# Attention multiplied in place in the sums' banks, the FFN's residual in halves, and the second load of x issued one batch ahead

## The chip, the cores and the metric

The kernel runs on one core of one Trainium2 chip. Its metric is the device time of one launch in microseconds (us), the median of three runs. Besides, one launch was recorded by the profiler, and all the rows in this document come from such recorded executions. The engines are called PE (TensorE, matrix products), DVE (VectorE), ACT (ScalarE), POOL (GpSimd) and SP (SyncE, which here only issues transfers). SBUF is the on-chip memory for operands. PSUM holds the matrix products, in 8 banks of 128 x 512 float32 values each.

## The reference: what is computed

One transformer layer on 32 batches of 512 tokens with 256 features: linear attention with 16 heads, and then a feed-forward network (FFN) with quantized weights. Each half has a layer norm in front and a residual around it. Cut to what matters:

```
q, k = elu(xn @ Wq.T + bq) + 1, elu(xn @ Wk.T + bk) + 1     # xn = layernorm(x)
v    = xn @ Wv.T + bv
num  = masked(q @ k.T) @ v + q @ S          # within chunks of 128, plus the state S so far
den  = sum(q * (cumsum(k) + z))             # per head and token
x1   = x + (num / den) @ Wo.T + bo
y    = silu((layernorm(x1) * gamma + beta) @ w1 + b1)        # w1, w2 dequantized; 256 -> 1024
out  = x1 + 0.5 * (y @ w2 + b2)                             # 1024 -> 256
```

## The kernel before, in words

One loop iteration works on three batches at once: the attention of batch i, the projections (k, q, v and the denominators) of batch i + 1, and the FFN of batch i - 1. The layer norm of batch i + 2's input is prepared too. Iterations 1 to 29 are a hardware loop; iterations 0, 30, 31 and 32 stand beside it as straight code with parts left out (32 is the last FFN alone).

Each engine has its own program, written out by hand as a list of calls: `pe_iteration`, `ve_iteration`, `ac_iteration`, `po_iteration` and `sp_iteration`. An engine carries its list out strictly in order. Between engines, an `Event` is a semaphore counted up when an instruction is done, and `w.need(event, shift, k)` makes the next instruction wait for that event of the batch `i + shift`. The order on each engine and these waits are all that sets the time.

Every matrix product is split into high and low parts, to be exact in float32: for an operand, ACT makes the high part (`..._hi`, a copy to the type FP32R) and DVE or POOL the low part (`..._lo`, the difference). Each stage passes through a PSUM bank. Which one is in the table `BANKS` (one entry per use, in TensorE's order). `free_bank` makes PE wait until the last use of the same bank has been read, and `FREED_BY` says by what.

The steps that the change and the prediction speak of:

- **Attention.** PE sums `num` in banks 0 and 1 (`values`, `from_states`). `reciprocals` makes 1/den, and eight transfers by SP (`sp_reciprocals`, L1049) spread it over the partitions into `rb` in SBUF. `attention(t)` (L662, DVE) multiplies `num` by `rb` and writes `rb`, once for each half t. `attention_hi` (L916, ACT) and `attention_lo` (L705, DVE) split the product into `gt_hi` and `gt_lo`, the operands of the output projection.
- **FFN.** For each of the eight column blocks j: `ffn_scaled` (L830, ACT) and `ffn_sum` (L626, DVE) read two banks, `ffn_silu` (L838, ACT) applies silu, `ffn_hi` (L845, ACT) makes `s_hi`, and `ffn_lo` (L986, POOL) makes `s_lo`. The second product `fc2` waits for all eight `s_hi` and `s_lo`.
- **The FFN's residual.** `residual` (L683, DVE, four instructions) makes `res` from `x1`, `residual_bias` (L998, POOL) adds the bias, and `final` (L673, DVE) adds the product and writes `out_t`.
- **The input a second time.** SP loads batch i again (L1057) into `xb` once the old `x1` is complete. `input_bias` (L992, POOL) adds the bias of the output projection, and `add_residual` (L714, DVE) makes `x1`.
- **Norms.** `ve_norm_x` (L563 to L570, DVE) makes the statistics of the input for batch i + 2, `po_norm` (L976, POOL) its factor, `ve_x_hat` (L576, DVE) the normed input.
- **Features.** `features` (L597, DVE) makes `phi_k` and `phi_q` from the banks of k and q, `cumulate` (L606, DVE) the running sum of the keys.

In `pe_iteration`, the projections of k, q and v stand behind the FFN's first product; then come `output_projection(0)` and `(1)`, `fc2(0)`, `fc2(1)`, `denominators`, `fc2(2)`, `fc2(3)`. The names in `BANKS` for these are k0 to v1, wo0, wo1, z0 (two `fc2` each), den and z1.

## Time and profile before

| | us |
|---|---|
| median of 3 runs (1483.11 to 1488.25) | 1483.45 |
| the profiled execution's own time | 1479.71 |
| its span, first to last instruction | 1478.0 |
| PE busy | 1402.7 (95%) |
| DVE busy | 1155.6 (78%) |
| ACT busy | 1087.9 (74%) |
| POOL busy | 674.9 (46%) |

Busy time is counted per engine, from the start to the end of each instruction, without waits. The engines work side by side, so the sum means nothing; the share tells how much of the span the engine was free. Since matrix products overlap in the pipeline, the start of one to the start of the next is the better measure of what one costs PE. Time rows name the kernel's line (L986 is line 986), the engine, what is written and read (`s_lo<-silu_f,s_hi`), and in square brackets how long the engine was idle just before and what ended that.

### The profile page before, as it was taken

Reading aid. Unit: us, or ns where it says so; the run is one execution under the profiler, and the core shown is the slowest. Engines: PE = TensorE matmul, PEld = TensorE weight load, DVE = VectorE, ACT = ScalarE, POOL = GpSimd, SP = SyncE. Lnnn points to the kernel's source line nnn. Section 1 sums busy time; section 2 is a strip of 40 time slices with the busy share of each in tenths; the row PEclk is TensorE's granted clock in tenths of the full one; section 3 lists DMA queues with packets and bytes.
Section 4 is the critical chain, followed back from the end, with each engine's and each line's share of the span. In section 5 each row is a group of like instructions: output and inputs, shape, how many; then the busy total and the mean of one; then the engine's idle time right before and its main releaser. Section 6 shows DMA issues by size and latency. Waiting matters only on the chain.

```text
span 1478.0 us, 61027 instructions
## 1 busy us (share of the span) xinstructions
PE 1402.7 (95%) x25746; PEld 1234.7 (84%) x25746; DVE 1155.6 (78%) x2014; ACT 1087.9 (74%) x1789; POOL 674.9 (46%) x473
## 2 busy tenths in 40 slices
PE   7669999999999999999999999999999999999978
PEld 6558888888888888888888888888888888888867
DVE  5478788778878777878877878877787887787755
ACT  4267787777778777778777778877777877777753
POOL 2133554444455443455444355544445544435543
PEclk8789999999999999999999999999999999999999
DMA  5112012222111222201222211122211122221010
GB/s 150 46 44 58 16 43 55 57 57 57 34 29 50 57 57 57 56 14 44 57 57 57 57 19 43 52 57 57 57 43 24 47 57 57 57 57 19 27 45 29
DMA packets 93538, 72.09 MB, mean 49 GB/s; under 512 B 8768, under 2 KB 92992, under 8 KB 93504
## 3 DMA queue, kind: packets, MB, share of 16 engines
q1 hardware_dynamic: 92144, 71.59, 19.3%
q8 instruction: 26, 0.43, 0.1%
q10 hardware_dynamic: 1360, 0.01, 0.1%
q14 instruction: 8, 0.07, 0.0%
HBM read 38.03 MB, written 16.78 MB: 37 GB/s over the span
## 4 chain that ended last, share of the span: by engine, by line
PE 49%; issue 19%; DVE 15%; POOL 10%; ACT 6%; DVEq 1%; POOLq 0%; DMA 0%; ACTq 0%
PE sc L292 26%; POOL s_lo L986 9%; DVE res L683 5%; PE sc L416 3%; DVE gt_lo L705 3%; PE num L358 3%; DVE stats L563 3%; PE ring L429 2%; PE num L359 2%; ACT silu_f L830 2%; DVE silu_f L626 2%; ACT s_hi L845 1%; ACT silu_f L838 1%; PE num L474 1%; PE sc L331 1%
## 5 line engine op out<-in xcount | busy, mean ns | idle before, releaser
L986 POOL TENSOR_TENSOR s_lo<-silu_f,s_hi 128x512 fp32r<-128x512 f32 x256 | 351.1, 1387 | 472.8 <-ACT s_hi L845 471.4
L292 PE MATMUL sc<-w_hi,s_hi 128*128 128x256 f32 x992 | 285.9, 288 | 20.6 <-POOL s_lo L986 20.5
L292 PE MATMUL sc<-w_lo,s_hi 128*128 128x256 f32 x992 | 280.5, 283 | 0.0
L292 PE MATMUL sc<-w_hi,s_lo 128*128 128x256 f32 x992 | 280.3, 283 | 0.0
L292 PEld LDWEIGHTS sc<-w_hi,s_hi 128*128 128x128 f32 x992 | 189.8, 191 | 31.6 <-DVE phi_q L597 24.7
L838 ACT ACTIVATE silu_f<-silu_f 128x512 f32<-128x512 f32 x256 | 159.1, 622 | 58.0 <-DVE silu_f L626 57.8
L292 PEld LDWEIGHTS sc<-w_lo,s_hi 128*128 128x128 f32 x992 | 190.0, 192 | 0.0
L292 PEld LDWEIGHTS sc<-w_hi,s_lo 128*128 128x128 f32 x992 | 189.9, 191 | 0.0
L636 DVE TENSOR_TENSOR probs<-sc,causal 128x1024 f32<-128x1024 f32 x128 | 153.4, 1220 | 29.2 <-PE sc L416 29.2
L845 ACT ACTIVATE s_hi<-silu_f 128x512 fp32r<-128x512 f32 x256 | 160.9, 628 | 5.2
L626 DVE SCALAR_TENSOR_TENSOR silu_f<-sc,scale,silu_f 128x512 f32<-128x512 f32 x127 | 95.0, 748 | 88.8 <-ACT silu_f L830 86.7
L673 DVE SCALAR_TENSOR_TENSOR out_t<-sc,res 128x512 f32<-128x512 f32 x64 | 42.3, 662 | 97.4 <-PE sc L292 92.4
L683 DVE TENSOR_SCALAR res<-x,res_mul,res_add 128x256 f32<-128x256 f32 x128 | 118.4, 984 | 0.0
L886 ACT ACTIVATE hn<-x,hn_add,ln_rstd 128x256 f32<-128x256 f32 x128 | 66.7, 594 | 65.6 <-DVE hn_add L736 65.6
L1005 POOL TENSOR_TENSOR qk<-qk,phi_q 128x512 f32<-128x512 f32 x64 | 82.7, 1293 | 59.5 <-DVE phi_q L597 59.5
L446 PEld LDWEIGHTS num<-probs,v_pad 64*32 64x32 f32 x8192 | 85.5, 105 | 27.3 <-issue 27.3
L446 PE MATMUL num<-probs,v_pad 64*32 64x64 f32 x8192 | 97.1, 226 | 9.6 <-issue 9.5
L830 ACT ACTIVATE silu_f<-ring,bias,scale 128x512 f32<-128x512 f32 x93 | 71.7, 771 | 42.0 <-PE ring L359 42.0
L992 POOL TENSOR_TENSOR xb<-xb,bias_o 128x1024 f32<-128x1024 f32 x32 | 76.5, 2390 | 54.5 <-DMA xb<-in_x 54.5
L358 PE MATMUL sc<-gt_hi,w_q 128*128 128x512 f32 x222 | 96.4, 434 | 0.2 <-DVE probs L636 0.2
L976 POOL TENSOR_TENSOR rstd<-ve,minus_half 128x4 f32<-128x4 f32 x32 | 33.0, 1031 | 133.3 <-DVE ve L570 133.3
L606 DVE TENSOR_TENSOR_SCAN qk<-ones,phi_k 128x512 f32<-128x512 f32 x64 | 90.3, 1411 | 1.1
(195 smaller groups left out, 3908.8 us busy)
## 6 DMA issues: line engine op xcount, KB each, us to landing
x_in<-in_x SPq DMA_DIRECT2D x32, 512.0 KB, 4.5
rb<-den_rows SPq DMA_DIRECT2D x256, 64.0 KB
xb<-in_x SPq DMA_DIRECT2D x32, 512.0 KB, 5.1
out<-out_t SPq DMA_DIRECT2D x64, 256.0 KB, 4.2
probs<-in_q SPq DMA_DIRECT2D x2, 512.0 KB, 8.3
silu_f<-in_q SPq DMA_DIRECT2D x2, 512.0 KB, 6.3
res<-in_sc SPq DMA_DIRECT2D x1, 512.0 KB, 7.0
out_t<-in_sc SPq DMA_DIRECT2D x1, 512.0 KB, 9.1
```

The costliest lines, as they stand in the source:

```text
L292: last = e.matmul(target, a, b, start=(n == 0), stop=(n == 3 * len(pairs) - 1))
L358: e.matmul(bank_, w1_q[:, t, cols], gt_hi[:, t, :], start=True, stop=False)
L446: last = e.matmul(num[PW * g:PW * (g + 1), r, num_of(r, t, m)], v_pad[toks, r, m, t * PAIRS + g, 2 * odd:2 * odd + 2, :], probs[toks, t, g ...
L606: kcum.done(e.tensor_tensor_scan(qk[:, t, :], ones[:, 0:1].to_broadcast([P, S]), phi_k[:, t, :], 0.0, ALU.mult, ALU.add))
L626: f_b.done(e.scalar_tensor_tensor(out=slot, in0=ffn_bank(j, 1, A), scalar=scale_1[:, 1, j:j + 1], in1=slot, op0=ALU.mult, op1=ALU.add))
L636: masked.done(e.tensor_tensor(probs[:, t, 2 * h:2 * h + 2, :, :, :].rearrange("p g m a q -> p (g m a) q"), sc[:, 2 * h:2 * h + 2, :].rearr ...
L683: last = e.tensor_scalar(res[:, c, :], x1[:, c, :], res_mul[:, c:c + 1], res_add[:, c:c + 1], ALU.mult, ALU.add)
L830: f_a.done(e.activation(silu_f[:, j % SLOTS, :], use_bank(f"f{j}a"), ACT.Identity, bias=bias_1[:, j:j + 1], scale=scale_1[:, 0, j:j + 1]))
L838: silu.done(e.activation(slot, slot, ACT.Silu))
L845: sh.done(e.activation(s_hi[:, j, :], silu_f[:, j % SLOTS, :], ACT.Copy))
L986: sl.done(e.tensor_tensor(s_lo[:, j, :], silu_f[:, j % SLOTS, :], s_hi[:, j, :].bitcast(F32), ALU.subtract))
L1005: qkcum.done(e.tensor_tensor(qk[:, t, :], qk[:, t, :], phi_q[:, t, :], ALU.mult))
```

## The change

TensorE's list of calls stays the same. What changes is the banks its products go to, and the lists of the other four engines.

- `attention` becomes one instruction for both halves, which writes its product back into banks 0 and 1. `attention_hi` and `attention_lo` become one instruction each and read these banks. So banks 0 and 1 are free only after `attention_lo` (`num` is freed by `at_l`), and the next to take bank 0 is v0, no longer q1. `rb` isn't overwritten any more, so the transfers to it wait for `attention`.
- `residual` and `residual_bias` work by halves of two token blocks. `final(n)` waits for its half alone.
- On DVE, `attention` moves ahead of `ffn_sum(6)`, and the residual moves from ahead of `ffn_sum(6)` to behind `attention_lo`. `features`, `cumulate`, `add_residual`, `norm_factors` and `reciprocals` stand in another order.
- On POOL, `input_bias` moves from behind `ffn_lo(0)` to the front of the iteration, and `po_norm` from ahead of `ffn_lo(7)` to the end.
- On SP, iteration i no longer loads `xb` for batch i when it begins, but for batch i + 1 once both halves of x1 of batch i are written.
- On ACT, the `ffn_...` calls, `attention_hi` and the calls behind it stand in another order.

The banks, of which only these entries bear on what follows:

```
-            "wo0": (6,), "wo1": (5,), "z0": (4,), "den": (0,), "z1": (2,),
+            "wo0": (7,), "wo1": (2,), "z0": (5,), "den": (2,), "z1": (7,),
...
-            "xt0": (xt_l, 0), "xt1": (xt_l, 1), "kv": (summed, 0), "num": (attn, 1),
+            "xt0": (xt_l, 0), "xt1": (xt_l, 1), "kv": (summed, 0), "num": (at_l, 0),
```

With the rest of the table, wo1 takes the bank of k0 (free after `features(0)`), z0 still that of q0 (free after `features(1)`), and kt1 the bank that z1 had (free after `final(1)`).

The core of the diff (calls that were moved are given for DVE, POOL and SP):

```diff
-            def attention(t):
+            def attention():
...
-                by_chunk = rb[:, t, :].rearrange("p (m r q) -> p r m q", r=2, q=HALF)
-                attn.done(e.tensor_tensor(
-                    by_chunk, num[:, :, t * 2 * P:(t + 1) * 2 * P].rearrange("p r (m q) -> p r m q", q=HALF),
-                    by_chunk, ALU.mult))
+                attn.done(e.tensor_tensor(num_view, num_view, by_half(rb[:, :, :]), ALU.mult))
...
-                at_l.done(e.tensor_tensor(gt_lo[:, t, :], rb[:, t, :], gt_hi[:, t, :].bitcast(F32), ALU.subtract))
+                at_l.done(e.tensor_tensor(by_half(gt_lo[:, :, :]), num_view, by_half(gt_hi[:, :, :].bitcast(F32)),
+                                          ALU.subtract))
...
-                at_h.done(e.activation(gt_hi[:, t, :], rb[:, t, :], ACT.Copy))
+                at_h.done(e.activation(by_half(gt_hi[:, :, :]), num_view, ACT.Copy))
...
             ffn_sum(5)
-            residual()
+            attention()
             ffn_sum(6)
-            attention(0)
-            attention(1)
             ffn_sum(7)
...
-            attention_lo(0)
-            attention_lo(1)
+            attention_lo()
+            residual(1)
+            residual(0)
             if N2:
                 ve_norm_x(e, w, 2)
...
+            input_bias()
             ffn_lo(0)
-            input_bias()
...
-            residual_bias()
             ffn_lo(6)
-            if N2:
-                po_norm(e, w, 2)
+            residual_bias(0)
             ffn_lo(7)
             query_sums(0)
             query_sums(1)
+            residual_bias(1)
             ln2_factors()
+            if N2:
+                po_norm(e, w, 2)
...
-            if A:
-                w.need(e_x1, -1)
-                x_again.done(e.dma_start(xb[:, :, :], x_v[i]))
             if N:
+                w.need(e_x1, 0)
+                x_again.done(e.dma_start(xb[:, :, :], x_v[i + 1]))
                 sp_reciprocals()
```

DVE in the loop, from the FFN's sum 5 to the input's statistics, before (`REGISTER_ALU` and `ISA` rows only compute semaphore values and wait):

```order
L626 SCALAR_TENSOR_TENSOR silu_f<-sc,scale,silu_f 128x512
L683 TENSOR_SCALAR res<-x,res_mul,res_add 128x256 x4
L58 REGISTER_ALU x2
L626 SCALAR_TENSOR_TENSOR silu_f<-sc,scale,silu_f 128x512
L58 ISA
L662 TENSOR_TENSOR rb<-num,rb 128x2x4x64 x2
L58 REGISTER_ALU x2
L626 SCALAR_TENSOR_TENSOR silu_f<-ring,scale,silu_f 128x512
L705 TENSOR_TENSOR gt_lo<-rb,gt_hi 128x512 x2
L58 ISA
L563 BN_STATS stats<-x_in 128x6 x4
```

The same place on DVE with the change (line numbers are those of the changed kernel):

```order
L632 SCALAR_TENSOR_TENSOR silu_f<-sc,scale,silu_f 128x512
L58 ISA
L667 TENSOR_TENSOR num<-num,rb 128x1024
L58 REGISTER_ALU x2
L632 SCALAR_TENSOR_TENSOR silu_f<-ring,scale,silu_f 128x512
L58 REGISTER_ALU x2
L632 SCALAR_TENSOR_TENSOR silu_f<-sc,scale,silu_f 128x512
L708 TENSOR_TENSOR gt_lo<-num,gt_hi 128x2x8x64
L686 TENSOR_SCALAR res<-x,res_mul,res_add 128x256 x4
L58 ISA
L569 BN_STATS stats<-x_in 128x6 x4
```

The attention's product now comes first, and the residual's four instructions last, ahead of the statistics.

POOL in the loop, from the FFN's low part 5 to its low part 7, before:

```order
L986 TENSOR_TENSOR s_lo<-silu_f,s_hi 128x512
L58 REGISTER_ALU
L998 TENSOR_TENSOR res<-res,bias 128x1024
L58 REGISTER_ALU
L986 TENSOR_TENSOR s_lo<-silu_f,s_hi 128x512
L58 REGISTER_ALU x2
L976 TENSOR_TENSOR rstd<-ve,minus_half 128x4
L58 REGISTER_ALU
L986 TENSOR_TENSOR s_lo<-silu_f,s_hi 128x512
```

POOL with the change, from the residual's first half to the end of the iteration:

```order
L1002 TENSOR_TENSOR res<-res,bias 128x512
L58 REGISTER_ALU
L989 TENSOR_TENSOR s_lo<-silu_f,s_hi 128x512
L58 ISA x2
L1009 TENSOR_TENSOR qk<-qk,phi_q 128x512
L58 REGISTER_ALU x2
L1009 TENSOR_TENSOR qk<-qk,phi_q 128x512
L1002 TENSOR_TENSOR res<-res,bias 128x512
L58 ISA
L1017 TENSOR_TENSOR ln_rstd<-ln_in,minus_half 128x8
L58 REGISTER_ALU x2
L979 TENSOR_TENSOR rstd<-ve,minus_half 128x4
```

The power for the input's norm (`rstd`) no longer stands ahead of the last low part; half of the residual's bias does.

## Rows read from the trace of the kernel before

**Rows 1.** DVE in the loop, by time: start us, us, engine line op
```profile
699.60 0.96 DVE L654 RECIPROCAL den_rows<-num 128x128 f32<-128x128 f32 x1 [0.95 <-PE num L474]
...
743.37 0.96 DVE L654 RECIPROCAL den_rows<-num 128x128 f32<-128x128 f32 x1 [0.94 <-PE num L474]
```

**Rows 2.** Windows: length, busy us of each engine, PE clock, DMA
```profile
700.48:744.25 43.77, 42.87 (x802) 37.78 (x801) 35.58 (x64) 34.08 (x56) 20.78 (x15) 1.00 0.20 48
...
1434.57:1440.40 5.83, 5.83 (x28) 5.83 (x29) 0.99 (x2) 0.00 (x0) 1.08 (x1) 0.52 0.01 3
```

**Rows 3.** PE by time, end of the output projection and start of fc2
```profile
734.26 0.28 PE L292 MATMUL sc<-wo_hi,gt_hi 128*128 128x256 f32 x1
...
735.58 0.28 PE L292 MATMUL sc<-wo_hi,gt_lo 128*128 128x256 f32 x1
736.75 0.35 PE L292 MATMUL sc<-w_hi,s_hi 128*128 128x256 f32 x1 [0.90 <-POOL s_lo L986]
```

**Rows 4.** Waits over the whole span: us in total, times, longest
```profile
PEld sc L292 <- DVE phi_q L597: 24.7, 26, 1.1
PE sc L292 <- POOL s_lo L986: 20.5, 28, 0.9
...
DVE w_lo L1251 <- ACT w_hi L1139: 3.2, 1, 3.2
```

**Rows 5.** POOL by time in the same iteration
```profile
717.31 2.39 POOL L992 TENSOR_TENSOR xb<-xb,bias_o 128x1024 f32<-128x1024 f32 x1 [1.28 <-DMA xb<-in_x]
...
726.65 2.42 POOL L998 TENSOR_TENSOR res<-res,bias 128x1024 f32<-128x1024 f32 x1 [0.55 <-DVE res L683]
...
733.68 1.02 POOL L976 TENSOR_TENSOR rstd<-ve,minus_half 128x4 f32<-128x4 f32 x1 [3.36 <-DVE ve L570]
734.67 1.94 POOL L986 TENSOR_TENSOR s_lo<-silu_f,s_hi 128x512 fp32r<-128x512 f32 x1
```

**Rows 6.** DVE by time in the same iteration
```profile
722.62 3.95 DVE L683 TENSOR_SCALAR res<-x,res_mul,res_add 128x256 f32<-128x256 f32 x4
...
727.15 1.27 DVE L662 TENSOR_TENSOR rb<-num,rb 128x512 f32<-128x512 f32 x2
...
729.12 2.35 DVE L705 TENSOR_TENSOR gt_lo<-rb,gt_hi 128x512 fp32r<-128x512 f32 x2
731.39 1.39 DVE L563 BATCH_NORM_STATS2 stats<-x_in 128x6 f32<-128x256 f32 x4
...
734.31 1.23 DVE L606 TENSOR_TENSOR_SCAN qk<-ones,phi_k 128x512 f32<-128x512 f32 x1
735.45 0.73 DVE L597 SCALAR_TENSOR_TENSOR phi_q<-sc,bias_qk,clip 128x512 f32<-128x512 f32 x1
```

**Rows 7.** Single lines, whole span: ns min/median/max
```profile
L683 DVE TENSOR_SCALAR res<-x,res_mul,res_add x128: 400/978/1522, 108.8 to 1461.1; 128x256 f32<-128x256 f32 x128
...
L705 DVE TENSOR_TENSOR gt_lo<-rb,gt_hi x64: 677/1732/1886, 68.3 to 1432.8; 128x512 fp32r<-128x512 f32 x64
...
L636 DVE TENSOR_TENSOR probs<-sc,causal x128: 1214/1221/1225, 47.8 to 1417.5; 128x1024 f32<-128x1024 f32 x128
```

**Rows 8.** ACT by time in the same iteration
```profile
724.62 0.77 ACT L830 ACTIVATE silu_f<-ring,bias,scale 128x512 f32<-128x512 f32 x1
...
728.47 1.14 ACT L916 ACTIVATE gt_hi<-rb 128x512 fp32r<-128x512 f32 x2
```

**Rows 9.** DMA issues: count, KB each, us to landing
```profile
xb<-in_x SPq DMA_DIRECT2D x32, 512.0 KB, 5.1
```

**Rows 10.** Iteration 31 by time, DVE
```profile
1431.05 3.47 DVE L705 TENSOR_TENSOR gt_lo<-rb,gt_hi 128x512 fp32r<-128x512 f32 x2 [0.28 <-ACT gt_hi L916]
```

**Rows 11.** Iterations 31 and 32 by time, POOL
```profile
1432.26 3.39 POOL L986 TENSOR_TENSOR s_lo<-silu_f,s_hi 128x512 fp32r<-128x512 f32 x2
...
1468.29 2.42 POOL L998 TENSOR_TENSOR res<-res,bias 128x1024 f32<-128x1024 f32 x1
```

**Rows 12.** Iteration 31 by time, PE
```profile
1434.57 0.58 PE L292 MATMUL ring<-wo_hi,gt_hi 128*128 128x256 f32 x1 [5.90 <-DVE gt_lo L705]
```

More of the change, by code:

```diff
@@ L225, in build @@
         F_ = dict(early=1)
-        res_m, e_res = ev("res_m", 1, **F_), ev("e_res", 1, **F_)
+        res_m, e_res = ([ev(f"{name}{h}", 1, **F_) for h in range(2)] for name in ("res_m", "e_res"))
         ht_pe, ht_h, ht_l = ev("ht_pe", T, **F_), ev("ht_h", T, **F_), ev("ht_l", T, **F_)
@@ L675, in final, with residual @@
                     in1=res[:, cs, :].rearrange("p c d -> p (c d)"), op0=ALU.mult, op1=ALU.add))
-            def residual():
-                if not Fn:
+            def residual(h, shift=-1):
+                if not (A if shift == 0 else Fn):
                     return
-                w.need(res_c, -1)
-                w.need(e_out, -2)
-                for c in range(C):
+                w.need(res_c, shift)
+                w.need(e_out, shift - 1, h)
+                for c in range(2 * h, 2 * h + 2):
                     last = e.tensor_scalar(res[:, c, :], x1[:, c, :], res_mul[:, c:c + 1], res_add[:, c:c + 1],
                                            ALU.mult, ALU.add)
-                res_m.done(last)
+                res_m[h].done(last)
             def ffn_input_lo(t):
@@ L785, in ve_iteration @@
             ffn_sum(5)
-            residual()
+            attention()
             ffn_sum(6)
-            attention(0)
-            attention(1)
             ffn_sum(7)
@@ L792, in ve_iteration @@
                 preparation[3]()
-            attention_lo(0)
-            attention_lo(1)
+            attention_lo()
+            residual(1)
+            residual(0)
             if N2:
@@ L992, in input_bias, with residual_bias @@
                 e_xb.done(e.tensor_tensor(xb[:, :, :], xb[:, :, :], bias_o[:, None, :].to_broadcast([P, C, D]), ALU.add))
-            def residual_bias():
-                if not Fn:
+            def residual_bias(h, shift=-1):
+                if not (A if shift == 0 else Fn):
                     return
-                w.need(res_m, -1)
-                e_res.done(e.tensor_tensor(res[:, :, :], res[:, :, :], bias_2[:, None, :].to_broadcast([P, C, D]), ALU.add))
+                w.need(res_m[h], shift)
+                cs = slice(2 * h, 2 * h + 2)
+                e_res[h].done(e.tensor_tensor(res[:, cs, :], res[:, cs, :], bias_2[:, None, :].to_broadcast([P, 2, D]), ALU.add))
             def query_sums(t):
```

72 lines of the change are left out of this document (37 added, 35 removed), and 8 rows, old and new, of the table BANKS.

## Prediction, written before the result was known

> **What bounds the kernel now.** I read four views. First the period of the loop: the same DVE instruction, the reciprocal, starts at 699.60 and at 743.37, so one batch takes 43.77 us [rows 1]. In that window PE is busy for 42.87 us, DVE for 35.58 [rows 2]. PE bounds the loop, and only what shortens PE's waits can shorten it; its products stay as they are. Second, PE by time, to find where it waits: the last product of the output projection starts at 735.58 and takes the usual 0.12 us (from 734.26 to 735.58 are eleven such steps), so PE was free at 735.70. The FFN's second product starts at 736.75 [rows 3]. That is a hole of 1.05 us. Third, the waits over the whole span, to see that the hole is there in each batch: 28 times, ended by the last `s_lo` from POOL, and 26 times its weight load waited for `phi_q` [rows 4]. They are one hole, seen from the load and from the product.
>
> Fourth, POOL and DVE by time, for why both are late. POOL's last `s_lo` starts at 734.67, behind the power `rstd` (1.02 us), which waited for the input's statistics on DVE; it takes 1.94 us and ends at 736.61 [rows 5]. DVE goes from 722.62 to 736.18 without a gap worth naming: residual 3.95, attention, `gt_lo` 2.35, statistics, features, running sum; `phi_q`, which frees the bank of z0, ends at 735.45 + 0.73 = 736.18 [rows 6]. To close the hole, both chains must end before 735.70: the first is 0.91 us late, the second 0.48.
>
> **A lock between DVE and POOL.** The residual's instruction takes 400 ns at least and 978 in the median, `gt_lo` 677 and 1732 [rows 7]. Both work from SBUF to SBUF, and both stand beside POOL's `s_lo`. `probs`, which reads PSUM, is never slower than 1225 ns for 1024 elements, whatever POOL does [rows 7]. So such a DVE instruction waits until the POOL instruction at hand has ended, and one with its first operand in PSUM doesn't. The same lock the other way made the last `s_lo` 1.94 long: the running sum held DVE's side from 734.31 [rows 5, 6].
>
> **The change part by part**, in the time of this batch.
>
> *Attention in place.* Two instructions, 1.27 us together, become one of 1024 elements: 1.2 us by `probs` [rows 6, 7]. No row shows DVE writing to PSUM. Below it could save the 0.1 us of one start; above I take twice the row, 2.4. I use 1.2, since the reading is the same. It stands ahead of the residual and of sums 6 and 7 now, so it starts when the state products are done, near 722.6, and ends near 723.8 (725.0 at most). ACT's one `gt_hi`, 1.14 us for both halves [rows 8], must follow `ffn_scaled(7)`, which ended at 725.39 [rows 8]: 726.5. DVE's sums 6 and 7 (0.7 each) lie in this gap, with either cost.
>
> *`gt_lo` from PSUM.* 2.35 us with the lock [rows 6] become 1.2 without it: 726.5 to 727.7. Before it was done at 731.47, so banks 0 and 1 are free long before v0 is reached. Cost on PE: none. v0 starts twelve steps of 0.12 times three ahead of 734.26, near 729.9, which leaves 2.2 us of cover.
>
> *Residual behind `gt_lo`.* It is moved from ahead of the sums to ahead of the statistics, so all of it is on the chain to `phi_q`. Free of POOL it costs 4 x 0.35 = 1.4 us (400 ns each, overlapped). POOL has only `s_lo` 5 and 6 left then; after these it waits for this residual itself. At most two waits of 1.3 us: 4.0. I take 3.1, between the two and nearer the 3.95 of before, and it ends at 730.8 (729.1 to 731.7).
>
> *To `phi_q`.* From the statistics' start at 731.39 to 736.18 are 4.8 us [rows 6], unchanged. 730.8 + 4.8 = 735.6 (733.9 to 736.5). PE is ready at 735.70. wo1 now needs `phi_k`, some 2 us earlier: 733.6 against 734.26. The hole from this side is closed, with 0.1 us of cover at my value, and up to 0.8 us stay at the upper end.
>
> *POOL.* Half of the residual's bias is 1.2 us (of 2.42) and `s_lo` 1.3: 730.8 + 2.5 = 733.3; if the running sum comes first, up to 1.2 more. That is before 735.70. The power `rstd` is behind it and is late for nobody: only `x_hat` needs it. `input_bias` (2.39 us, for which POOL had waited 1.28 [rows 5]) leaves the row of `s_lo`, so sums 4 and 5 are no longer held by full slots. This is off the chain, because attention waits for PE's state products anyway.
>
> *Second load of x.* It is issued when x1 is complete, at about 739 to 740, lands 5.1 us later [rows 9] and is used on POOL at once. SP has nothing else to issue there: the transfers of `rb` come behind it, at the reciprocal's end near 744. The load costs nothing; the 2.39 us on POOL now lie beside `x_hat`.
>
> By the Trainium skill, SBUF — State Buffer, "SBUF: two separate sides", the port pair that DVE and GpSimd share is locked for a whole instruction and the loser fully blocks. The trace agrees in kind, with the 400 and 978 ns above; that `x_hat` will meet `input_bias` there is a rival below.
>
> *The ends.* In iteration 31 PE waits 5.90 us for `gt_lo`, which the lock stretches to 3.47 and which ends at 1434.52 [rows 10, 12]. Now it ends near 1431.1 (attention at 1426.6, one `gt_hi`, one `gt_lo`), 3.4 us earlier. But the last `s_lo` waits for half a residual: 1431.1 + 3.3 + 1.2 + 1.3 = 1436.9, after the 1435.65 of before [rows 11]. From there three `fc2` of 2.88 us end near 1445.6, where before 1448.6. This gives 3.0 us. Behind the wait PE ran at a granted clock of 0.52 for 5.83 us [rows 2]; a shorter wait may save up to 3 us of that, which I leave in the range. In the last FFN half the residual's bias leaves the chain: 1.2 us (of 2.42 [rows 11]). At the start the split of w2 stands behind the norm's factors, so a DVE wait of 3.2 us [rows 4] no longer delays them: 0 to 2 us, of which I count none.
>
> **Sum.** 28 batches x 1.05 = 29.4, plus 3.0, plus 1.2: 33.6 us. 1479.71 - 33.6 = 1446.1 for an execution like the profiled one. The median is 3.7 us above that execution, which gives 1483.45 - 33.6 = 1450. Between these bounds lies the forecast's own range: with 28 x 1.1 and all of the ends (3.0 + 3 + 1.2 + 2) 40 us, 1443; with 28 x 0.8 and 3 of the ends 25 us, 1458.
>
> **Rivals.**
>
> *The chain to `phi_q` takes over.* If the residual meets both `s_lo`, or ACT runs later than I have it, `phi_q` ends at 736.0 to 736.6 and PE starts 0.5 us before its old time, not 1.05. For it: my cover is 0.1 us. Against: ACT's `ffn_scaled(7)` and `gt_hi` have fewer calls ahead of them than the times I used. 28 x 0.5 + 4 = 18: 1465. Nearly the same comes of the lock beside `x_hat`: `input_bias` may hold it until about 747.7, `x_hat` ends at 749.1, and `final(1)`, which frees kt1's bank now, is 0.5 us late. For it: the order on POOL. Against: `x_hat` was over 3 us ahead of `final(1)`.
>
> *No change.* A new bank or order stops PE elsewhere for the whole 1.05 us, for instance f2a, which waits for sum 0, now one `xt_lo` (0.6 us) later. Against: each of these has cover of some tenths. 1483.45 less the ends: 1479.
>
> *Slower.* DVE's write into PSUM is dear. Sums 6, 7 and `gt_lo` then wait for it. Its place is the start of `gt_lo`, 722.6 + a + 1.4; from a = 2.6 us on each us counts in full (at 2.5 it meets the 726.5 above), from 3.7 the old hole is filled again. At four times the row, 4.9 us, a batch takes 1.2 us longer: 28 x 1.2 - 4 = 30 us, 1513. For it only that no row shows such a write.
>
> **Chances.** Forecast 0.66; half 0.18; no change 0.09; slower 0.07. The range for 8 in 10 takes the forecast's own and most of the half case: 1443 to 1468. A measurement of this kernel tells about 0.5% from no change, 7.4 us. Faster by over that: 0.66 + 0.18 = 0.84; within it 0.09; slower 0.07.
>
> **What would show it.** Right: the reciprocal comes every 42.7 us; no wait row of PE for `s_lo` with 28 counts; `gt_lo` is one instruction of about 1.2 us, and attention too; the residual's four stand ahead of the statistics and take 1.4 to 4.0 us; `input_bias` runs near 744 to 747 with no wait for its transfer behind an `s_lo`. Wrong: PE waits before fc2 for `phi_q` (first rival), before kt1 for `out_t` (lock at `x_hat`), or DVE's product into `num` takes over 2.6 us. If the period stays 43.7 with all of these short, my reading of the hole was wrong.

## The result, and the profile after

The changed kernel takes 1433.35 us in the median of 4 runs (1428.62 to 1437.86); the kernel before took 1483.28 beside it (1480.40 to 1488.25, 4 runs). The ratio is 0.966, with a 95% interval of 0.964 to 0.968: 3.4% faster. I had forecast 1450 with a range from 1443 to 1468. The sign is right, and the time lies 10 us below the lower end.

| | before | after |
|---|---|---|
| the profiled execution's own time | 1479.71 | 1433.77 |
| its span | 1478.0 | 1432.0 |
| PE busy | 1402.7 (95%) | 1395.5 (97%) |
| DVE busy | 1155.6 (78%) | 1146.0 (80%) |
| ACT busy | 1087.9 (74%) | 1081.8 (76%) |
| POOL busy | 674.9 (46%) | 662.9 (46%) |

To find where 46.0 us of span went I used landmarks that both kernels have: DVE's first reciprocal, which ends the prologue, and `hn_add`, which comes once a batch. First the kernel before, DVE by time (start us, us, engine line op):

```profile
41.18 0.96 DVE L654 RECIPROCAL den_rows<-num 128x128 f32<-128x128 f32 x1 [4.75 <-PE num L474]
...
86.44 0.16 DVE L736 SCALAR_TENSOR_TENSOR hn_add<-mv,ln_rstd 128x4 f32<-128x4 f32 x1 [0.89 <-POOL ln_rstd L1013]
...
219.52 0.15 DVE L736 SCALAR_TENSOR_TENSOR hn_add<-mv,ln_rstd 128x4 f32<-128x4 f32 x1
...
1356.83 0.15 DVE L736 SCALAR_TENSOR_TENSOR hn_add<-mv,ln_rstd 128x4 f32<-128x4 f32 x1
...
1402.53 0.15 DVE L736 SCALAR_TENSOR_TENSOR hn_add<-mv,ln_rstd 128x4 f32<-128x4 f32 x1
```

Then the same landmarks of the changed kernel (the 1st, 4th, 30th and 31st `hn_add` in both):

```profile
32.05 0.96 DVE L660 RECIPROCAL den_rows<-sc 128x128 f32<-128x128 f32 x1 [4.34 <-PE sc L480]
...
74.79 0.16 DVE L741 SCALAR_TENSOR_TENSOR hn_add<-mv,ln_rstd 128x4 f32<-128x4 f32 x1 [1.76 <-POOL ln_rstd L1017]
...
205.72 0.16 DVE L741 SCALAR_TENSOR_TENSOR hn_add<-mv,ln_rstd 128x4 f32<-128x4 f32 x1 [1.91 <-POOL ln_rstd L1017]
...
1313.41 0.17 DVE L741 SCALAR_TENSOR_TENSOR hn_add<-mv,ln_rstd 128x4 f32<-128x4 f32 x1 [1.91 <-POOL ln_rstd L1017]
...
1357.74 2.34 DVE L741 SCALAR_TENSOR_TENSOR hn_add<-mv,ln_rstd 128x4 f32<-128x4 f32 x1 [1.76 <-POOL ln_rstd L1017]
```

| stretch | before | after | gain | forecast |
|---|---|---|---|---|
| prologue, to the first reciprocal | 41.18 | 32.05 | 9.1 | not in the sum |
| from there to the 1st `hn_add` (iteration 0) | 45.26 | 42.74 | 2.5 | 0 (0 to 2) |
| 30 batches, to the 31st `hn_add` | 1316.09 | 1282.95 | 33.1 | 29.4 |
| from there to the end (iterations 31 and 32) | 75.47 | 74.26 | 1.2 | 4.2 |
| sum | 1478.0 | 1432.0 | 46.0 | 33.6 |

In the middle of the loop, between the 4th and the 30th `hn_add`, a batch took (1356.83 - 219.52) / 26 = 43.74 us and takes (1313.41 - 205.72) / 26 = 42.60. This "us a batch" is the measure in all that follows. In the period below PE now has no wait left; the row has busy time for PE, PEld, DVE, ACT and POOL, then the granted clock, the DMA share and GB/s (before: [rows 2]):

```profile
700.12:742.70 42.58, 42.58 (x802) 37.81 (x801) 35.15 (x61) 33.88 (x56) 20.49 (x15) 1.00 0.20 49
```

The next fence is the changed kernel by time, DVE from `gt_lo` to `phi_q`, then the attention product of the batch behind it, then POOL beside them. It answers to [rows 5, 6].

```profile
700.12 1.23 DVE L708 TENSOR_TENSOR gt_lo<-num,gt_hi 128x1024 fp32r<-128x1024 f32 x1
701.26 2.82 DVE L686 TENSOR_SCALAR res<-x,res_mul,res_add 128x256 f32<-128x256 f32 x4
...
707.53 1.23 DVE L612 TENSOR_TENSOR_SCAN qk<-ones,phi_k 128x512 f32<-128x512 f32 x1
708.67 0.73 DVE L603 SCALAR_TENSOR_TENSOR phi_q<-sc,bias_qk,clip 128x512 f32<-128x512 f32 x1
...
739.49 1.23 DVE L667 TENSOR_TENSOR num<-num,rb 128x1024 f32<-128x1024 f32 x1 [0.79 <-PE num L466]
...
702.24 1.36 POOL L989 TENSOR_TENSOR s_lo<-silu_f,s_hi 128x512 fp32r<-128x512 f32 x1 [0.26 <-ACT s_hi L849]
704.15 1.31 POOL L1002 TENSOR_TENSOR res<-res,bias 128x512 f32<-128x512 f32 x1 [0.55 <-DVE res L686]
705.52 1.29 POOL L989 TENSOR_TENSOR s_lo<-silu_f,s_hi 128x512 fp32r<-128x512 f32 x1
```

PE behind them, the last product of the output projection and the first on `s_hi`:

```profile
709.74 0.28 PE L298 MATMUL sc<-wo_hi,gt_lo 128*128 128x256 f32 x1
709.86 0.28 PE L298 MATMUL sc<-w_hi,s_hi 128*128 128x256 f32 x1
```

They follow one another at the usual 0.12 us. `phi_q` ends at 709.40, 0.46 us ahead of it, and the last `s_lo` at 706.81, 3.05 us ahead. Before, both were late, and PE stood for 1.05 us. The in-place product writes PSUM in 1.23 us, the price that I had read from `probs`. In the waits over the whole span, where [rows 4] had 28 waits for `s_lo` and 26 for `phi_q`, PE's waits ahead of that product are down to one, in iteration 31:

```profile
PE sc L298 <- POOL s_lo L989: 0.9, 1, 0.9
```

The prologue is the surprise. Before, by time, ACT, then DVE and PE:

```profile
29.91 1.20 ACT L875 ACTIVATE v_pad<-num 64x512 f32<-64x512 f32 x2 [7.08 <-PE num L292]
31.14 0.69 ACT L853 ACTIVATE clip<-num,bias_qkm 128x512 f32<-128x512 f32 x1
...
32.52 0.75 DVE L597 SCALAR_TENSOR_TENSOR phi_q<-num,bias_qk,clip 128x512 f32<-128x512 f32 x1 [8.49 <-ACT clip L856]
...
40.03 1.08 PE L474 MATMUL num<-qk,head_one 128*32 128x128 f32 x16 [8.42 <-POOL qk L1005]
```

After, the same steps:

```profile
22.42 0.69 ACT L857 ACTIVATE clip<-sc,bias_qkm 128x512 f32<-128x512 f32 x1
...
29.06 1.20 ACT L879 ACTIVATE v_pad<-num 64x512 f32<-64x512 f32 x2 [4.07 <-PE num L298]
...
23.80 0.75 DVE L603 SCALAR_TENSOR_TENSOR phi_q<-sc,bias_qk,clip 128x512 f32<-128x512 f32 x1 [0.19 <-ACT clip L860]
...
31.34 0.64 PE L480 MATMUL sc<-qk,head_one 128*32 128x128 f32 x16 [0.17 <-POOL qk L1009]
```

ACT's list of the loop also runs in the prologue. There `values_out(0)` waits 7.08 us for v's product. PE isn't idle in that time: between the products of q and v it makes 36 small ones that occur only there (L1264 and L1270, 22.64 to 26.99), and then those of v at 0.21 us each where the loop has 0.12. Before the change the last `exponential` stood behind this wait, though the product that it reads had ended at 22.8. It now stands ahead: its `clip` starts at 22.42 instead of 31.14.

The end got shorter in one place and longer in another. In iteration 31 PE waits 2.59 us for `gt_lo`, not 5.90 [rows 12], and in the 5.83 us behind that wait the granted clock is 0.73 instead of 0.52 [rows 2]. In the last FFN PE waits for the first `s_hi`, and then runs at a lower granted clock. PE by time, and the window behind the wait (busy PE, granted clock, DMA share, GB/s):

```profile
1385.88 0.58 PE L298 MATMUL ring<-wo_hi,gt_hi 128*128 128x256 f32 x1 [2.59 <-DVE gt_lo L708]
...
1409.45 0.54 PE L392 MATMUL sc<-w_hi,s_hi 128*128 128x256 f32 x1 [1.92 <-ACT s_hi L849]
1409.79 0.41 PE L394 MATMUL sc<-w_lo,s_hi 128*128 128x256 f32 x1
...
1409.50:1414.00 4.50, 4.50 (x21) 0.62 0.02 5
```

From PE's transposes of the last batch to the end of the span are 29.37 us before (from 1448.63) and 32.02 after:

```profile
1399.98 1.04 PE L346 MATMUL num<-ident,hn 128*128 128x128 f32 x8
```

### The profile page after: what moved, and what is told of

Same layout as the page of the kernel before. It is cut to its first block and busy times, and to the rows that moved or that the text cites. A ratio compares the mean times of both kernels' runs of the same rounds, so it can differ in the third digit from the quotient of the medians.

```text
span 1432.0 us, 61029 instructions
## 1 busy us (share of the span) xinstructions
PE 1395.5 (97%) x25746; PEld 1236.2 (86%) x25746; DVE 1146.0 (80%) x1950; ACT 1081.8 (76%) x1757; POOL 662.9 (46%) x505
## 5 line engine op out<-in xcount | busy, mean ns | idle before, releaser
L298 PE MATMUL ring<-w_hi,s_hi 128*128 128x256 f32 x496 | 143.4, 289 | 0.0
L298 PE MATMUL sc<-w_hi,s_hi 128*128 128x256 f32 x496 | 140.4, 283 | 0.9 <-POOL s_lo L989 0.9
L298 PE MATMUL sc<-w_lo,s_hi 128*128 128x256 f32 x496 | 140.4, 283 | 0.0
L298 PE MATMUL sc<-w_hi,s_lo 128*128 128x256 f32 x496 | 140.2, 283 | 0.0
L298 PE MATMUL ring<-w_hi,s_lo 128*128 128x256 f32 x496 | 140.2, 283 | 0.0
L298 PE MATMUL ring<-w_lo,s_hi 128*128 128x256 f32 x496 | 140.2, 283 | 0.0
L834 ACT ACTIVATE silu_f<-sc,bias,scale 128x512 f32<-128x512 f32 x124 | 96.7, 780 | 42.5 <-PE sc L365 36.6
L834 ACT ACTIVATE silu_f<-ring,bias,scale 128x512 f32<-128x512 f32 x93 | 72.6, 780 | 38.2 <-PE ring L365 33.6
L298 PEld LDWEIGHTS ring<-w_hi,s_hi 128*128 128x128 f32 x496 | 94.8, 191 | 6.0 <-issue 6.0
L298 PEld LDWEIGHTS sc<-w_hi,s_hi 128*128 128x128 f32 x496 | 95.2, 192 | 1.1 <-issue 1.1
L298 PEld LDWEIGHTS sc<-w_lo,s_hi 128*128 128x128 f32 x496 | 95.2, 192 | 0.0
```

Source lines behind the costliest of these rows:

```text
L298: last = e.matmul(target, a, b, start=(n == 0), stop=(n == 3 * len(pairs) - 1))
L834: f_a.done(e.activation(silu_f[:, j % SLOTS, :], use_bank(f"f{j}a"), ACT.Identity, bias=bias_1[:, j:j + 1], scale=scale_1[:, 0, j:j + 1]))
```

## Experiments

Names that begin with `b_` are the kernel before with one edit, those with `a_` the changed kernel with one edit. "First rec." is the start of the first reciprocal, "a batch" the measure from above, "last FFN" the stretch from PE's last `hn` transposes to the end. Single profiled executions differ: the changed kernel, once more as `after_again`, and two variants that leave its loop's lists alone (`a_list_start`, `a_tail`) gave 42.60 to 42.68 us a batch. A difference under 0.1 is no finding by itself. The first reciprocal scatters too, by more than a microsecond (31.92 to 33.30 in the changed kernel and its variants but `a_list_start`). The times were taken in several comparisons; the kernel before had medians of 1483.3 to 1491.9 in them, so the ratio to it is the safer column, and the trace decides between theories.

| kernel | first rec. | a batch | last FFN | median us | ratio to before |
|---|---|---|---|---|---|
| before | 41.18 | 43.74 | 29.37 | 1483.28 | 1 |
| after | 32.05 | 42.60 | 32.02 | 1433.35 | 0.966 [0.964, 0.968] |
| `after_again` | 32.07 | 42.67 | 32.29 | 1437.46 | 0.968 [0.965, 0.970] |
| `a_list_start` | 40.36 | 42.65 | 32.26 | 1445.48 | 0.967 [0.964, 0.971] |
| `a_list_loop` | 32.25 | 42.62 | 32.50 | 1436.43 | 0.962 [0.958, 0.965] |
| `b_exp3` | 33.84 | 43.75 | 29.38 | 1475.67 | 0.989 [0.985, 0.993] |
| `b_rstd_last` | 41.42 | 43.77 | 29.35 | 1483.43 | 0.993 [0.990, 0.995] |
| `a_rstd_early` | 33.29 | 42.62 | 32.41 | 1437.32 | 0.963 [0.960, 0.967] |
| `a_res_early` | 33.21 | 42.85 | 31.06 | 1441.98 | 0.966 [0.963, 0.969] |
| `a_attn_rb` | 31.92 | 42.73 | 31.14 | 1441.47 | 0.967 [0.963, 0.970] |
| `b_order` | 41.94 | 42.78 | 30.12 | 1456.91 | 0.976 [0.973, 0.980] |
| `b_res_late` | 42.24 | 42.75 | 30.06 | 1455.37 | 0.980 [0.977, 0.983] |
| `a_wlo_early` | 33.30 | 42.63 | 32.50 | 1439.53 | 0.970 [0.967, 0.973] |
| `a_tail` | 32.19 | 42.68 | 29.54 | 1434.73 | 0.967 [0.964, 0.969] |

`after_again` is the changed kernel without an edit.

> The changed kernel once more, unchanged, beside the others of this comparison: the level that the experiments on it are held against where the kernel before took 1490 us rather than 1483. Expected: first reciprocal at 32 to 33 us, 42.60 us a batch, 1433 to 1438 us.

It came out at 1437.46 us, within that, and 4.1 us above its first median; in the loop the two differ by 0.07 us a batch.

### The prologue: ACT's list

`a_list_start`:

```diff
+            if not A:      # the prologue
+                values_out(0); exponential(3); table_silu(); values_out(1); q_by_parity(0)
+            else:
                 exponential(3); q_by_parity(0); values_out(0); values_out(1); table_silu()
```

> The kernel after the change, with ScalarE's list as it was before in the prologue alone (v's product into v_pad ahead of the last exponential); loop and end as after the change. Theory (the start was the missed term): before the change that copy waited for PE until 29.91 us, phi_q of the last column block came at 32.52 and the first reciprocal at 41.18; after it the reciprocal came at 32.05. The first reciprocal goes back to about 41.2 and the time is 9.1 us above the changed kernel (about 1442; bounds 8 to 10). Rival (the start is shorter because of the banks or of the weights' lower halves, not of the list): the reciprocal stays at 32 and the time within 1 us of the changed kernel.

The first reciprocal goes back to 40.36, 8.3 us later than in the changed kernel, and the time is 8.0 us above that of `after_again`, which ran in another comparison, and 9.1 above that of `a_list_loop`, which ran in the same one. The rival is out.

`a_list_loop` is the same with `if A:` (the loop and not the prologue).

> The kernel after the change, with ScalarE's list as it was before in every iteration with attention (v's copy ahead of the last exponential, q by parity last), the prologue as after the change. Theory: in the steady iteration the product of v is done some 2 us after the last qk product, the last exponential comes about 1.5 us later and the last phi_q ends well before the first matmul on s_hi, so nothing waits: within 1.5 us of the changed kernel (1432 to 1435). Rival (part of the loop's gain came from this list: the chain exponential, phi_q, x_hat had 1 us less): 0.5 to 1.0 us a batch, 15 to 30 us more (about 1448 to 1463).

42.62 us a batch, the prologue at 32.25, 1436.43 us: in the loop this order is worth nothing that can be seen. The same few calls are worth 8 to 9 us in the prologue and nothing in the loop.

`b_exp3`:

```diff
-            values_out(0)
             exponential(3)
+            values_out(0)
```

> The kernel before, with one swap in ScalarE's list: the last exponential ahead of v's first copy. Theory: the first reciprocal moves from 41.18 to about 32, and nothing else changes, since in the loop the copy of v at the head of the queue did not wait: 9 us less than before, about 1474. Rival: the loop gains too (phi_q is one of the two that end the hole ahead of fc2, up to 0.1 us a batch, 3 us more): 1471. Second rival: the start does not move, 1483.

The first reciprocal starts at 33.84, 7.3 us earlier than before where I expected 9, and a batch takes 43.75: the theory holds in kind. The span is 10.0 us shorter (1468.0). Besides the 7.3 these are 1.1 in the 30 batches and 2.1 behind them, less 0.5 in iteration 0, where the swap has no known effect. By the medians the kernel is 16 us faster than before, but the kernel before spread over 17 us in that comparison (1480.68 to 1497.67), and of the 16 the trace shows 10, of which 7.3 are the swap's.

### The loop: which move closes the hole

`b_rstd_last`:

```diff
-            if N2:
-                po_norm(e, w, 2)
             ffn_lo(7)
             query_sums(0)
             query_sums(1)
             ln2_factors()
+            if N2:
+                po_norm(e, w, 2)
```

> The kernel before, with GpSimd's power for rstd moved from ahead of the last s_lo to the end of its list. Theory (the hole of 1.05 us ended by the later of two chains): the last s_lo comes 0.4 us earlier and no longer beside the scan, so the hole is then ended by the last phi_q, which ended 0.57 us before the end of the hole; 0.5 us a batch, 28 batches, 14 us less than before (about 1469; bounds 1465 to 1475). Rival (s_lo alone made the hole, phi_q was never needed at that place): the whole 1.05 us, about 1454. Rival (the power only trades places: x_hat comes late instead and PE waits for its transposes): within 3 us of 1483 or above.

43.77 us a batch: nothing gained. It is not what any theory said, since the x_hat that the third one feared is early. The rows show a fourth way (DVE, POOL and PE by time, one batch):

```profile
737.28 1.55 DVE L606 TENSOR_TENSOR_SCAN qk<-ones,phi_k 128x512 f32<-128x512 f32 x1
738.75 0.72 DVE L597 SCALAR_TENSOR_TENSOR phi_q<-sc,bias_qk,clip 128x512 f32<-128x512 f32 x1
...
736.45 1.30 POOL L986 TENSOR_TENSOR s_lo<-silu_f,s_hi 128x512 fp32r<-128x512 f32 x1 [3.16 <-ACT s_hi L845]
...
739.53 0.39 PE L292 MATMUL sc<-w_hi,s_hi 128*128 128x256 f32 x1 [0.67 <-DVE phi_q L597]
```

The last `s_lo` now runs at its 1.30 us and is done at 737.75. But it got hold of the shared side first, and DVE's running sum took 1.55 us instead of 1.23 [rows 6]. Counted from the start of the product with the states (720.66 before, 723.44 here), `phi_q` ends after 16.03 us where it ended after 15.52, and the product on `s_hi` starts after 16.09 in both. Of the 0.51 us by which `phi_q` is later, the running sum accounts for 0.32. The other 0.2 were there when the residual began (1.96 us after the start of the states' product before, 2.16 here), and they lead to what starts the whole chain.

**The head of the chain: the second load of x.** DVE's row without a gap begins with the residual, which follows sum 5. Sum 5 waits for ACT's `ffn_scaled(5)`, this for a slot that POOL's `s_lo` frees, and the `s_lo` stand behind `input_bias`, which waits for the second load of x. Two batches of the kernel before, one short and one long (DVE's reciprocal, POOL's `input_bias`, and in the long one ACT's `ffn_scaled(5)` and PE's first product of q1):

```profile
611.51 0.96 DVE L654 RECIPROCAL den_rows<-num 128x128 f32<-128x128 f32 x1 [0.94 <-PE num L474]
628.98 2.40 POOL L992 TENSOR_TENSOR xb<-xb,bias_o 128x1024 f32<-128x1024 f32 x1 [1.04 <-DMA xb<-in_x]
...
654.98 0.96 DVE L654 RECIPROCAL den_rows<-num 128x128 f32<-128x128 f32 x1 [0.94 <-PE num L474]
673.57 2.40 POOL L992 TENSOR_TENSOR xb<-xb,bias_o 128x1024 f32<-128x1024 f32 x1 [2.21 <-DMA xb<-in_x]
...
677.29 0.78 ACT L830 ACTIVATE silu_f<-sc,bias,scale 128x512 f32<-128x512 f32 x1 [1.21 <-POOL s_lo L986]
...
684.71 0.50 PE L292 MATMUL num<-xt_hi,wq_hi 128*128 128x512 f32 x1 [0.65 <-DVE rb L662]
```

In the first, `input_bias` starts 17.47 us behind the reciprocal and the batch takes 43.47; in the second 18.59 and 44.62 (to the reciprocal at 699.60 [rows 1]). So it is in all of the 26 batches that I compared in the loop: `input_bias` waits for the load each time, it starts 17.2 to 18.6 us behind the reciprocal, and the batch ends 26.05 us after it, to within 0.12. The batch takes as long as the load is late. SP issues it (at 667.55 in the long batch) only behind the eight transfers of `rb`, which follow the reciprocal, so the chain from one reciprocal to the next closes on itself. In late batches PE waits for its end in two places, before q1 for `attention` and before fc2. With the power moved (`b_rstd_last`) the distance is 25.89 us, 0.16 less, but the load landed 0.17 us later in the mean of that execution, and the two cancel. In the changed kernel `input_bias` no longer waits for its load in these batches: it starts 0.7 us behind the reciprocal, and 25 of 26 batches take 42.57 to 42.72 us. This chain is read from the traces; that the load's place alone would close the hole is not shown.

So the power's place is worth 0.16 us a batch at an equal landing, not the 0.5 expected: the lock took back what it had given to `s_lo`. The ratio of 0.993 [0.990, 0.995] has the same wide spread of before as in `b_exp3`; 0.16 us in 30 batches is 5 us of the 8 to 11 that it stands for, if the landings are equal. The profiled execution has a span of 1481.7, 3.7 above the profiled one of before.

`b_res_late` moves the residual behind `gt_lo` on DVE and its bias behind the query sums on POOL, and leaves the power ahead of the last `s_lo`:

```diff
             ffn_sum(5)
-            residual()
             ffn_sum(6)
...
             attention_lo(1)
+            residual()
...
-            residual_bias()
             ffn_lo(6)
...
             query_sums(1)
+            residual_bias()
```

(`add_residual` waits for the residual too, since x1 is read later.)

> The kernel before, with the residual behind gt_lo on DVE and its bias behind the query sums on GpSimd, the power for rstd where it was, ahead of the last s_lo. Known so far, per batch in the middle of the loop: before 43.74, power alone moved 43.77, both moved 42.78, changed kernel 42.60. Theory (the residual's place is the whole of it: it held back sums 6 and 7 and with them s_lo, and took 3.9 instead of 2.8 us beside s_lo): 42.8 to 42.9 a batch. Rival (two chains end the hole together and each alone gives nothing): above 43.3 a batch.

`b_order` has both moves.

> The kernel before, with the order of the change alone on two engines: residual behind gt_lo on DVE (and add_residual waiting for it), its bias behind the query sums on GpSimd, the power for rstd last. Attention product in rb, banks, ScalarE's list, transfers as before. Theory: sums 6 and 7 and s_lo come 3 to 4 us earlier, so the last s_lo has reserve; phi_q is still behind gt_lo of 2.35 us, and the residual behind gt_lo takes 2.8 instead of 3.9: phi_q ends 0.5 to 1.1 us before where it did (15.52 us after the product with the states), and the hole is 0 to 0.5 us: 15 to 29 us less than before (1454 to 1468). Rival (only the attention product in place opens the hole's chain): under 5 us less (1478 to 1483).

42.75 and 42.78 us a batch: the rival of 43.3 is out. The residual's place gives 0.99 us of the 1.14, and the power's place nothing that can be seen on top. By time, `b_res_late`:

```profile
717.27 1.97 DVE L705 TENSOR_TENSOR gt_lo<-rb,gt_hi 128x512 fp32r<-128x512 f32 x2 [0.20 <-ACT gt_hi L917]
719.17 1.37 DVE L683 TENSOR_SCALAR res<-x,res_mul,res_add 128x256 f32<-128x256 f32 x4
...
724.52 0.73 DVE L597 SCALAR_TENSOR_TENSOR phi_q<-sc,bias_qk,clip 128x512 f32<-128x512 f32 x1
...
722.75 1.02 POOL L977 TENSOR_TENSOR rstd<-ve,minus_half 128x4 f32<-128x4 f32 x1 [4.66 <-DVE ve L570]
723.74 1.96 POOL L987 TENSOR_TENSOR s_lo<-silu_f,s_hi 128x512 fp32r<-128x512 f32 x1
...
725.86 0.34 PE L292 MATMUL sc<-w_hi,s_hi 128*128 128x256 f32 x1
```

The four residual instructions take 1.37 us, where they took 3.95 [rows 6]: no `s_lo` runs beside them any more. So DVE reaches `phi_q` earlier, and with it the variance, the power and the last `s_lo`, which all hang on DVE's queue. `phi_q` ends at 725.25 and `s_lo` at 725.70, 0.6 and 0.16 us before PE's product on `s_hi`, which keeps its usual step of 0.12. The cover of `s_lo` is next to nothing: in the kernel before, where PE waited for it, PE started 0.14 us behind its end. One move that shortens DVE's queue takes both chains out. But the load still heads the chain, and where it lands late the hole is back: in `b_res_late` the two batches whose `input_bias` started 18.2 us behind the reciprocal took 43.2 us, and in `b_order` the batches took 42.5 to 43.5, the longest where it started at 18.6. The holes left on average, 0.05 and 0.11 us, are a third and a half of what the two take more than the changed kernel.

`a_rstd_early` puts the power back ahead of the last `s_lo` in the changed kernel, `a_res_early` the residual ahead of the attention product:

```diff
 # a_rstd_early, POOL
+            if N2:
+                po_norm(e, w, 2)
             ffn_lo(7)
...
 # a_res_early, DVE
             ffn_sum(5)
+            residual(1)
+            residual(0)
             attention()
             ffn_sum(6)
...
             attention_lo()
-            residual(1)
-            residual(0)
```

> The kernel after the change, with GpSimd's power for rstd back ahead of the last s_lo. In the changed kernel the last s_lo ends at about 706.8 us of the middle iteration, the first matmul on s_hi starts at 709.86 and DVE's variance ends at 706.84. Theory (the place of the power is not what counts once DVE is early): the power ends near 707.8, the last s_lo at 709.1 to 710.0 beside a scan: 0 to 0.3 us a batch, 0 to 8 us in all (1433 to 1441). Rival (the power ahead of s_lo alone makes the hole of the kernel before): about 1 us a batch, 30 us more (1463).

42.62: as the theory said, and the rival of 1 us a batch is out.

> The kernel after the change, with DVE's four residual instructions back ahead of the attention product (both halves, in the order they have). Theory: they come beside two or three s_lo (3.9 us for the four in the kernel before against 2.8 behind gt_lo), so phi_q ends 1.1 us later than 709.40 where the matmul on s_hi starts at 709.86: a hole of about 0.65 us; and sums 6 and 7 with their silu, s_hi and s_lo come 3 to 4 us later against a reserve of 3.0 us: a hole of up to 1 us. 0.65 to 1.0 us a batch, 20 to 31 us in all (1453 to 1464). Rival (order on DVE is of no matter, the gain is from the one wide attention product and gt_lo): under 5 us (1433 to 1438).

42.85, that is 0.2 us a batch or some 6 us where I expected 20 to 31. The direction is right, the size is not. PE's product on `s_hi` started 0.05 us behind the end of `phi_q`, and in all 26 batches 0.26 to 0.28 us behind the product before it, instead of 0.12: a small hole, ended by `phi_q`. The residual took 3.19 us beside the `s_lo`, not 3.95, and the last `s_lo`, which I had thought late too, was early. This says more than a miss: with the residual back in its old place, the rest of the change (the load among it) still gives 0.89 of the 1.14 us. Either the residual's move alone or the rest without it nearly closes the hole, so the gain can't be shared out between them. What the load's new place gives alone is open.

`a_attn_rb` lets the wide attention product write to `rb`, and `gt_hi` and `gt_lo` read from there:

```diff
-                attn.done(e.tensor_tensor(num_view, num_view, by_half(rb[:, :, :]), ALU.mult))
+                attn.done(e.tensor_tensor(by_half(rb[:, :, :]), num_view, by_half(rb[:, :, :]), ALU.mult))
```

> The kernel after the change, with the attention product written to rb (SBUF) instead of in place into the banks; gt_hi and gt_lo read rb, and the reciprocals' transfers wait for gt_lo again. Theory: the difference gt_lo then has both inputs in SBUF and takes 2.35 us beside s_lo as in the kernel before, instead of 1.23; phi_q ends 1.1 us later, 0.65 us past the start of the matmul on s_hi: 20 us in all (1453). Rival (the slow gt_lo of before came from its two instructions' place beside s_lo and not from where the operand lies, or the reserve is larger): under 4 us (1433 to 1437).

42.73 us a batch, 0.05 to 0.13 more than the changed kernel, not 0.65. Writing the attention's product in place is worth 1.5 to 4 us of 33, at the edge of what can be told. By time:

```profile
701.00 1.23 DVE L708 TENSOR_TENSOR gt_lo<-rb,gt_hi 128x1024 fp32r<-128x1024 f32 x1
702.14 3.33 DVE L686 TENSOR_SCALAR res<-x,res_mul,res_add 128x256 f32<-128x256 f32 x4
...
709.95 0.73 DVE L603 SCALAR_TENSOR_TENSOR phi_q<-sc,bias_qk,clip 128x512 f32<-128x512 f32 x1
...
701.56 3.11 POOL L989 TENSOR_TENSOR s_lo<-silu_f,s_hi 128x512 fp32r<-128x512 f32 x2 [2.02 <-ACT s_hi L849]
...
710.74 0.39 PE L298 MATMUL sc<-w_hi,s_hi 128*128 128x256 f32 x1
```

`gt_lo` reads two SBUF tiles and still takes 1.23 us, because it started before the `s_lo`. It is the `s_lo` that waits: two of them take 3.11 us (1.30 each elsewhere), and the residual behind them 3.33 instead of 2.82. So the lock costs 0.5 us here, behind `gt_lo` rather than in it. That uses up the cover of `phi_q`: PE's product on `s_hi` starts 0.06 us behind its end, and 0.15 to 0.17 us behind the product before it in every batch instead of 0.12.

### Iteration 0 and the last FFN

`a_wlo_early` splits the first half of w2's lower part ahead of `add_residual(1)` again, and the second behind the norm factors:

```diff
+            if preparation[1]:
+                preparation[1](0)
             add_residual(1)
             norm_x1()
             norm_factors()
             if preparation[1]:
-                preparation[1](0)
                 preparation[1](1)
```

> The kernel after the change, with the first half of w2's lower part split ahead of add_residual(1) in iteration 0 and the second half behind the norm factors, as before. Theory: iteration 0's norm factors wait again for ScalarE's w2_hi (3.2 us on DVE before the change), and the distance from the first reciprocal to the first hn_add goes from 42.7 back towards 45.3: 1 to 3 us more than the changed kernel. Rival (iteration 0 is set by PE's lower clock there): within 0.5 us.

From the first reciprocal to the first `hn_add` are 45.2 us (33.30 to 78.47). That would be the 2.4 us of the theory, but the changed kernel itself has 42.7 in one execution and 44.7 in the other (32.07 to 76.77 in `after_again`). In iteration 0 PE's granted clock changes from stretch to stretch, and this spread is as large as the effect. In the changed kernel and its other variants the stretch took 40.8 to 44.7 us, in the kernel before and its variants 45.3 to 46.1; with the split back it is the longest of the changed ones. So a gain of iteration 0 is there, but whether the split or the clock gave it is open.

`a_tail`, the last iteration of ACT's list (A is false and Fn true there only):

```diff
             ffn_silu(0)
             ffn_scaled(2)
+            if Fn and not A:
+                for j in range(FT):
+                    if j:
+                        ffn_silu(j)
+                    ffn_hi(j)
+                return
             ffn_silu(1)
             ffn_hi(0)
```

> The kernel after the change, with ScalarE's list in the last iteration (the FFN of the last batch alone) silu(j), s_hi(j) in turn for j = 0 to 7, as the kernel before had it there; all else as after the change. Theory: there s_hi(0) stood behind silu(1), which waits for the sum of tile 1; PE waited 1.9 us for it and then ran 4.5 us at a granted clock of 0.62. The stretch from PE's transposes of that batch to the end goes from 32.0 us to 29.4, as in the kernel before: 2.6 us less than the changed kernel (1 to 3.5). Rival (the stretch is longer because the residual beside the s_lo takes 4.4 instead of 3.3 us): under 0.7 us.

The stretch is 29.54 us against 32.02 and 32.29. PE by time at the place where the changed kernel had its wait of 1.92 us, and the window behind it:

```profile
1410.28 0.39 PE L392 MATMUL sc<-w_hi,s_hi 128*128 128x256 f32 x1
1410.50 0.28 PE L394 MATMUL sc<-w_lo,s_hi 128*128 128x256 f32 x1
...
1410.30:1414.80 4.50, 4.34 (x30) 1.00 0.02 5
```

The product starts on time, and the clock stays at 1.00. The rival is out. By time `a_tail` has 1434.73 us (1434.00 to 1435.42), and the changed kernel beside it, `after_again`, 1437.46 (1434.27 to 1439.93): 2.7 us less, as expected, though the two sets of four runs touch.


## Why the prediction was right in sign and wrong in size

**What bounds the kernel: right as to the hole, wrong as to its head.** The hole before fc2 came with each batch, and it was closed. The period was to be 42.7 us and is 42.58 in the profiled window, where PE has no wait: PE bounds the changed kernel. But I began DVE's chain at 722.62 and did not ask what had started it. That was the landing of the second load of x, by way of `input_bias`, and the length of each batch followed it to within 0.12 us. The prediction calls the new place of `input_bias` "off the chain"; in the kernel before it was on it, and PE waited for a chain that closed on itself through SP's queue. In the changed kernel, with the load gone from there, `attention` does wait for PE, as the prediction says (0.79 us).

**The sum for the loop: nearly right, for a partly wrong reason.** I priced the hole at 1.05 us and multiplied by the 28 waits that the trace listed. In the loop's middle a batch gained 1.14, and the gain came in 30 batches, not 28: 33.1 instead of 29.4. Of the missing 3.7 us, two more batches are some 2; the waits before q1 in batches with a late load are 0.1 us a batch on average, which I had not counted. Of the 0.1 to 0.2 us a batch between `b_order` and the changed kernel about half is late landings, the rest stays unexplained. The reason: I let two moves close two chains, the power's place the one of `s_lo`, the residual's place and the attention's the one of `phi_q`. The runs show one move doing both: the residual alone gives 0.99. The power's place gives 0.16 in the kernel before, hidden there by the later load, and nothing in the changed kernel. And the residual's move was not the only way: `a_res_early`, without it, keeps 0.89.

**`gt_lo` "become 1.2 without it": right number, wrong cause.** `a_attn_rb` has the 1.23 us from SBUF as well. My reading of [rows 7] was "a DVE instruction from SBUF waits for POOL"; what counts is who starts first. The Trainium skill says just this, SBUF — State Buffer, "SBUF: two separate sides": whichever of the two starts first holds the pair for the whole instruction. I had used the half of the rule on the loser. The traces agree: two `s_lo` that took 3.11 us instead of 2.6, held up by a `gt_lo` that started 0.56 us earlier in `a_attn_rb`, the running sum stretched by an earlier `s_lo` in `b_rstd_last`.

**The residual at 3.1 us: right enough** (2.82, bounds 1.4 to 4.0), and `phi_q` was ready 0.46 us ahead where I had given it 0.1.

**The start: the step that failed.** The change's list for ACT was passed over as "another order", and the prologue has no term in the sum: of the start the prediction prices only the split of w2, at 0 to 2 us, "of which I count none". The prologue gave 9.1 us, more than two thirds of the 12.4 by which the sum of 33.6 is short, and nearly all of the distance from the range's lower end of 1443 to the measured 1433.35. `a_list_start` takes 8.3 us of it back by ACT's list alone, and `b_exp3` gives the kernel before 7.3 by one swap. The trace of before had it in plain rows, a wait of 8.42 us of PE for POOL at 40.03 and one of 7.08 of ACT at 29.91. They were waits outside the loop, and I looked for waits that repeat. Iteration 0 gave another 2.5 us where I counted none; its cause stays open.

**The end: 1.2 us for the forecast 4.2.** Up to PE's last transposes the gain is 3.9 us (from the 31st `hn_add`: 46.10 before, 42.24 after) for a forecast of 3.0: the wait for `gt_lo` fell by 3.3 us, the one for the last `s_lo` behind it was 0.88, and PE was back at its higher clock sooner, which the prediction had left in the range. The last FFN was to give 1.2 and cost 2.65. ACT's list, which helped the prologue, has `s_hi(0)` behind `silu(1)`. Undone in `a_tail`, 2.5 us come back. Both errors, 9.1 us gained and 2.65 lost that the sum doesn't have, are one: a list that three stages share was read in the loop only.

**From the execution to the median.** I added the 3.7 us by which the median of before lay above the profiled run. After, the two agree within 0.4 us: the lift did not carry over, and 3.7 of the forecast's distance to the measured median is that.

**The rivals.** "Slower by a dear write into PSUM" is refuted by the 1.23 us. The lock beside `x_hat` did come true (2.80 us for its four instructions against 1.3 alone) and cost nothing: `final(1)` behind it still waited 0.70 us for PE, and PE's transposes of `x_hat` came 4.5 us after its end.

## What to carry to other kernels

When a list of calls serves the prologue, the loop and the last iteration, read a change of it in each of them: calls that are hidden in the loop stood in front of a wait of 7 us in the prologue and made one of 1.9 us at the end. When two chains end in one hole, look for the queue that feeds both; shortening one of them alone can lengthen the other. Then follow that queue back to what starts it, here a load: batches that differ in length show it, since the head of the chain moves with them. And an instruction that competes with another engine's is best moved to where that engine is idle: the four residual instructions cost 3.95 us in one place and 1.37 in another.

## What the runs showed of the hardware

- The wait between DVE and POOL on SBUF operands goes both ways, and the one that starts first keeps its normal time. A running sum (`tensor_tensor_scan`) of 128x512 takes 1.23 us alone and 1.55 beside an `s_lo` that began first; two `s_lo` take 3.11 us where a `gt_lo` began first, 2.6 alone; four 128x256 `tensor_scalar` take 1.37 us with POOL idle and mostly 3.9 to 4.0 where POOL's `s_lo` ran beside them.
- DVE's product in place in two PSUM banks, 128x1024 in fp32, took 1.23 us, the same as from PSUM to SBUF (1.23 in `a_attn_rb`).
- PE's wait of 1.92 us in the last FFN was followed by 4.5 us at a granted clock of 0.62, a mean of the two levels 1.2 and 2.4 GHz: the products came every 0.21 us, then every 0.12. Without the wait (`a_tail`) the clock stayed at 1.00. The wait and what followed thus cost 2.5 us in all.
